# Rows of a DRAM scratch laid out for reads of 8 KB, written by 16 transfers in place of one

## The reference

```
def step(h, inp):
    x_t, dt_t, B_t, C_t = inp
    dA = jnp.exp(dt_t[..., None] * A)
    h = dA * h + (dt_t * x_t)[..., None] * B_t[:, :, None, :]
    y = jnp.einsum('bgpn,bgn->bgp', h, C_t)
    return (h, y)
```

## Time and profile before

| | |
|---|---|
| median of 3 runs | 1326.49 us (1325.91 to 1327.89) |
| the profiled execution | 1327.35 us, its span 1325.6 us |
| TensorE busy | 1094.1 us, 83% |
| VectorE busy | 1101.3 us, 83% |
| GpSimd busy | 977.7 us, 74% |
| ScalarE busy | 626.5 us, 47% |
| DMA packets | 99512, 98784 of them under 8 KB |
| mean granted TensorE clock | 0.919 |

### The profile page before, as it was taken

One profiled execution on the slowest core, in us unless ns is written; L12 is line 12 of the kernel. 1 busy time (PEld: TensorE's weight loads), 2 busy tenths in 40 slices (PEclk: granted clock), 3 DMA queues, 4 the chain that ended last, 5 costly groups with the idle time before them and its releaser, 6 DMA issues.

```text
span 1325.6 us, 14750 instructions
## 1 busy us (share of the span) xinstructions
PE 1094.1 (83%) x3848; PEld 551.6 (42%) x3848; DVE 1101.3 (83%) x1265; ACT 626.5 (47%) x1070; POOL 977.7 (74%) x596
## 2 busy tenths in 40 slices
PE   2476658999798987999698987999698988998888
PEld 1121123445344453435344453445344454445445
DVE  3389998899889998999889998999989998997222
ACT  3645455445554455545554454545554355442310
POOL 0489997877879786877888786877888788875100
PEclk9776779999899997999899997999899998999889
DMA  5797866655665657575756647574756557550000
GB/s 194 175 236 157 186 153 133 141 131 124 161 143 128 143 134 162 119 158 118 170 133 138 140 119 167 122 167 103 177 129 145 118 132 167 127 127 32 1 0 17
DMA packets 99512, 176.56 MB, mean 133 GB/s; under 512 B 12960, under 2 KB 21600, under 8 KB 98784
## 3 DMA queue, kind: packets, MB, share of 16 engines
q1 hardware_dynamic: 98272, 171.36, 56.2%
q0 software_dynamic: 1152, 4.19, 0.9%
HBM read 150.34 MB, written 8.39 MB: 120 GB/s over the span
## 4 chain that ended last, share of the span: by engine, by line
PE 34%; POOL 27%; issue 21%; ACT 7%; DVE 6%; DMA 3%; SPq 1%; POOLq 0%; DVEq 0%; ACTq 0%
POOL h_s L980 16%; PE p_r L456 9%; PE p_r L467 6%; PE p_r L462 6%; POOL bt_s L960 5%; PE p_dt L411 4%; PE p_y L422 3%; PE p_r L442 2%; DVE h_s L760 2%; DMA bt_s<-dx_rows 2%; PE p_r L473 2%; PE p_r L437 1%; ACT p_dt L549 1%; POOL carry L977 1%; POOL sp_l L994 1%
## 5 line engine op out<-in xcount | busy, mean ns | idle before, releaser
L980 POOL TENSOR_TENSOR h_s<-h_s,c_s 128x1024 f32<-128x1024 f32 x256 | 608.3, 2377 | 127.5 <-DVE h_s L760 117.2
L549 ACT ACTIVATE p_dt<-p_dt,an_s 128x512 f32<-128x512 f32 x512 | 333.1, 657 | 334.0 <-PE p_dt L411 333.5
L411 PE MATMUL p_dt<-kdt,pick_s 128*128 128x512 f32 x512 | 357.6, 704 | 106.9 <-DVE h_s L760 105.0
L760 DVE TENSOR_TENSOR_SCAN h_s<-p_dt,carry,bt_s 128x512 f32<-128x512 f32 x256 | 322.2, 1272 | 25.3 <-ACT p_dt L549 20.3
L760 DVE TENSOR_TENSOR_SCAN h_s<-p_dt,bt_s 128x512 f32<-128x512 f32 x256 | 304.9, 1210 | 31.0 <-ACT p_dt L549 17.7
L467 PE MATMUL p_r<-nT,w_s 128*128 128x512 f32 x512 | 243.2, 602 | 0.4 <-ACT nT L686 0.4
L960 POOL TENSOR_TENSOR bt_s<-bt_s,b_s 128x1024 f32<-128x1024 f32 x96 | 226.7, 2361 | 10.9 <-DMA bt_s<-dx_rows 10.5
L411 PEld LDWEIGHTS p_dt<-kdt,pick_s 128*128 128x128 f32 x512 | 103.4, 204 | 264.8 <-DVE h_s L760 180.7
L745 DVE TENSOR_TENSOR bt_s<-bt_s,p_b 128x1024 f32<-128x1024 f32 x160 | 192.7, 1204 | 4.5 <-issue 2.8
L456 PE MATMUL p_r<-nT,gu_s 128*128 128x512 f32 x352 | 169.4, 602 | 0.3 <-DVE th_s L905 0.3
L422 PE MATMUL p_y<-h_s,ysel_s 128*32 128x512 f32 x1024 | 150.6, 663 | 18.8 <-POOL h_s L980 18.8
(11 more groups left out here) (93 smaller groups left out, 900.7 us busy)
## 6 DMA issues: line engine op xcount, KB each, us to landing
bt_s<-dx_rows SPq DMA_DIRECT2D x512, 256.0 KB, 5.3
kdt<-st_dt SPq DMA_DIRECT2D x64, 128.0 KB, 3.2
tok<-in_x SPq DMA_DIRECT2D x8, 512.0 KB, 7.1
xr_s<-xb_s SPq DMA_DIRECT2D x64, 64.0 KB, 2.4
dx_rows<-sp_w SPq DMA_DIRECT2D x16, 256.0 KB, 2.0
b_s<-xb_s SPq DMA_DIRECT2D x64, 64.0 KB, 2.5
xo<-in_x SPq DMA_DIRECT2D x8, 512.0 KB, 3.9
out<-xo POOLq DMA_DIRECT2D x8, 512.0 KB, 3.4
```

Source lines behind the costliest of these rows:

```text
L411: nc.tensor.matmul(p_dt[DT_BANK[u]][:, :], sel, kdt[:, h, p // 16, :], start=True, stop=True)\
L549: A(p_dt[DT_BANK[u]][:, :], p_dt[DT_BANK[u]][:, :], ACT.Exp, scale=an_s[:, c:c + 1]).then_inc(a_dA, 1)
L760: V.tensor_tensor_scan(h_s[:, u % 8, :], p_dt[DT_BANK[u]][:, :], bt_s[:, u % 16, :], carry[:, u:u + 1] if par else 0.0, ALU.mult, ALU.add) ...
L980: G.tensor_tensor(h_s[:, two, :], h_s[:, two, :], c_s[:, h, :].unsqueeze(1).broadcast_to([P, 2, T]), ALU.mult)\
```

## The change

The scratch has a further layout: for each group and each of eight runs of a half, the four channels of the run stand one behind another, 4 x 512 x 4 B = 8 KB. A read still goes to 32 partitions and moves 256 KB, but takes one piece of 8 KB for each partition in place of four pieces of 2 KB that lie 64 KB apart. The write must put the eight channels of each pair (a, g) into that order and becomes 16 DMAs of 8 partitions (every fourth partition of `sp_w`), 16 KB each, in place of one of 128 partitions. The counts of `l_rows` go from 16 to 256 for each half.

```
-        dx_rows = nc.dram_tensor("dx_rows", [2, 2, P, T], F32).ap()
+        dx_rows = nc.dram_tensor("dx_rows", [2, 2, GH, 8, 4 * T], F32).ap()
...
-                p = unit_channel(4 * r)
...
-                kept_rows, scanned = number((t * 2 + h + 1) * 16), number(t * U + 4 * r - 12)
+                kept_rows, scanned = number((t * 2 + h + 1) * 256), number(t * U + 4 * r - 12)
...
                 for g in range(GH):
-                    src = dx_rows[par, h].rearrange("(a b g) t -> g b a t", a=4, g=GH)[g, p]
-                    sp.dma_start(bt_s[NS * g:NS * g + NS, slot:slot + 4, :], src.partition_broadcast(NS))\
-                      .then_inc(l_dx[r % 4], 16)
+                    sp.dma_start(bt_s[NS * g:NS * g + NS, slot:slot + 4, :].rearrange("p a t -> p (a t)"),
+                                 dx_rows[par, h, g, r % 8].partition_broadcast(NS)).then_inc(l_dx[r % 4], 16)
...
                 sp.wait_ge(g_dx, t * 2 + h + 1)
-                sp.dma_start(dx_rows[par, h], sp_w[:, :]).then_inc(l_rows, 16)
+                for a in range(4):
+                    for g in range(GH):
+                        sp.dma_start(dx_rows[par, h, g, :, a * T:a * T + T], sp_w[32 * a + g:32 * a + 32:GH, :])\
+                          .then_inc(l_rows, 16)
...
-                        act.wait_ge(l_rows, m * 16)
+                        act.wait_ge(l_rows, m * 256)
```

## The result

The changed kernel takes 1380.08 us in the median of 4 runs, the kernel before 1326.45: ratio 1.0402, 95% interval 1.0384 to 1.0420. That is 53 us more (4.0%); the prediction said 17 (range to 1359). The direction and the places were right, the size that it gave was a third of the measured one. The profiled execution has a span of 1376.2 us, 50.6 more than before.

The account below looks back on a forecast made before the run. Bound: the chain through ScalarE's `res`, delayed by late `xo` in SyncE's queue, with TensorE gapless later. 4.0 us at the start plus 13.0 at ends of tiles, 17.0 on 1327.35, less 0.86, gives 1343.5 us; range 1330 to 1359.

Parts of the forecast that it names:

- the sensitive place: SyncE's queue between a tile's last `keep_rows` (write of `dx_rows`) and the load of `xo`; a delay there delays the tile.
- the first run: Start: first four reads issued 7.35 us later, landing at 59.5 against GpSimd's start at 55.6; 4 us lost.
- The price of an issue: SyncE's queue: 0.49 us for each write, so 16 hold it 7.7 us in place of 0.38, 7.35 us more.
- the dear bound: SyncE's queue: all 16 writes as dear as SBUF to SBUF, 0.64 us each, 9.8 us more each time.
- working at the ends of tiles: Second half's writes delay `xo`: 7.35 us less each body's margin; lost 4.75, 3.8, 0.4 and 4.05, sum 13.0 us.
- The gain of the reads: Start: pieces of 8 KB land 5.2 us after first issue in place of 8.6, gain 3.4 us or 0; steady state 0.
- The second wait at the start: GpSimd's 4.2 us wait for a run behind the second write and 2 MB of weights; later issue and quicker reads cancel, 0.
- The middle of a tile: First half's writes: the next run goes out 2 us late, but its landing leaves 8 us before GpSimd; term 0.
- A stall of ScalarE counts in full: Ends of tiles: every microsecond ScalarE waits for `xo` lengthens the run, as the chain passes there and TensorE has no gap later.
- C: Rival, dear issues or slow reads: 9.8 us a group gives 1362 us, slow reads alone 1354; chance 0.18.
- A: Rival, issues cheap or covered: no measurable change, 1326.5 or up to 1329 us (1335 with 5.7 us each); chance 0.11.
- B: Rival, faster: GpSimd's second wait for reads at the start goes, 4.2 us won, 1322.3 us; chance 0.08.

Follow-up runs that it names:

- e9_xo_early_after: The changed kernel with a buffer of its own for the output and `xo` loaded at u = 44 of the body before: 1348.02 us, ratio 1.0139.
- e2_reads8k: The kernel before with the new layout and reads of 8 KB alone, still one write of 128 partitions: ratio 0.9987.
- e5_spread: The changed kernel with the second half's loads and writes moved in SyncE's queue behind the load of `xo` and one run of reads: ratio 1.0064.
- e6_forms: The kernel before (old layout) with 16 writes of 16 KB for each half, in several shapes tile by tile: 1373.73 us in one run.
- e14_w1_128: Reads of 8 KB with single writes, each 1 MB run read from weights w1 by one DMA into 128 partitions, not from the scratch: 1318.25 us, one run.
- e15_w1_32: Reads of 8 KB with single writes, each 1 MB run read from weights w1 by four DMAs of 32 partitions: 1325.15 us, one run.
- e8_xo_early: The kernel before with a buffer of its own for the output and `xo` loaded at u = 44 of the body before: ratio 0.9984.

## Why the prediction was wrong, step by step

**What bounds the kernel, and the sensitive place: right.** Late `xo` behind the second half's writes (`e9_xo_early_after`), the first run at the start, and no waiter for reads in the steady part (`e2_reads8k`). Moving the steps in the queue takes most of the loss away with every write still issued (`e5_spread`).

**The price of an issue: the step that failed most.** I took 0.49 us from the one write of before, which stood alone, with 0.64 (the SBUF to SBUF row) as the dear bound. Measured: 604 ns and a gap, 0.65 us, 10.3 us more for each group in place of 7.35, so even my dear bound was passed. I had argued that the shape doesn't set the price, since a larger transfer was the cheaper; `e6_forms` shows that the shape sets it, from 0.33 to 0.65 us at the same 16 KB. The loss is steep in this price, as the prediction said. Its own working at the ends of tiles with 10.3: 7.7 for body 1, 9.7 for 3 and 5, 7.0 for 7 and, by the margins of 2, 4 and 6, 8.3 at most, 32.7 us, in place of 13.0. Measured 28.3. Body by body the two agree less well, in us:

| body | by the working, at 10.3 | ScalarE's wait for `xo` grew by | VectorE's copies shorter by | lost |
|---|---|---|---|---|
| 1 | 7.7 | 7.6 | 2.3 | 3.5 |
| 2 | 3.0 | 4.0 | 0.5 | 4.2 |
| 3 | 4.9 | 6.2 | 2.7 | 3.6 |
| 4 | 2.0 | 3.1 | 0.2 | 3.3 |
| 5 | 4.9 | 5.1 | 2.9 | 2.9 |
| 6 | 3.3 | 5.2 | 1.1 | 2.8 |
| 7 and 8 | 7.0 | 7.9 | none there | 8.1 |

"Lost" is how much further behind the changed kernel is at the write ahead of the next body. Body 1 lost less than half of the working's figure, bodies 2 and 4 lost more than theirs; that the sums come so near is in part luck.

**The gain of the reads: failed.** 3.4 us counted, none measured at the start (8.7 us from issue to use, before 8.6). The 5.2 us of `pick` were no price for longer pieces but for 128 partitions (`e14_w1_128`, `e15_w1_32`). The estimate of 3% less, which I had worked out from the Trainium skill (DMA: Bandwidth & Descriptors, "Why small descriptors are slow") and set aside, is near what the traces show: 730 us of the engines' time with the reads of 8 KB alone, 745 before, and a packet of 8 KB takes 612 ns in the median where four of 2 KB take 616.

**The second wait at the start, set to 0: failed.** I had let later issue and quicker reads cancel. Nothing was quicker, and the group that stands in front of the fourth run is a second one, on top of the late start: 13.4 us in place of 4.2, so 9.2, above the 7.35 that I had given as its worst. With 9.7 for the first run (4 predicted) and 3.5 in the middle of tile 0, the start lost 22.3 us in place of 4. Two other waits are new at the start: ScalarE's for the written rows (8.5 us, to 52.07) and TensorE's for `kdt` (8.2 us, to 55.23). Both end ahead of GpSimd's first multiplication at 65.33, as I had said of the first.

**The middle of a tile at 0: right but for tile 0.** There GpSimd waited 3.5 us at 168.88, where I had read the margin off body 4 only.

**A stall of ScalarE counts in full: only in part.** The wait grew by 39.1 us and 28.3 us were lost. VectorE's copies, which had waited for GpSimd, became 9.6 us shorter at the same places, and that covers most of the difference. In body 7, which has no such copies, the wait counts in full, 7.9 us against 8.1. Of the 21.2 us that were there before, little counted (`e8_xo_early`): half of them lie in body 8 beside the output projection, which I had not looked up.

**The sum.** With what was measured for each term, 17.0 becomes 32.7 at the ends of tiles, 9.7 for the first run, 9.2 for the second wait and 3.5 in tile 0: 55.1 us against the 50.6 by which the span grew. The price of an issue is the largest part of the miss.

**Rivals.** C (dear issues or slow reads) came true in both parts at once, which the prediction priced only one by one (1362 and 1354), and with the second wait on top; a range that takes in bounds of several unknown costs has to allow for their sum. A and B were ruled out. (In A, 5.7 - 3.4 is 2.3 us, not 2.4; nothing hangs on it.)

## What to carry to other kernels

A queue's issue time is a resource like an engine's: before cutting one DMA in many, find what stands behind it in the queue, and price an issue by a row of the same shape, or measure that shape by itself. Steps that can wait belong behind the ones that are waited for: the same 256 writes cost 53 us in one order and 8.5 in another. A wait in the profile isn't worth its length: look for what ends next, and at durations that are out of proportion with the size of the instruction.

## What the runs showed of the hardware

- An issue of 16 KB from SBUF to DRAM holds SyncE's queue for 0.33 us (8 neighbouring partitions), 0.45 to 0.48 (16 x 1 KB, 32 x 512 B, 128 x 128 B) or 0.65 us (8 partitions with a step of 4, 64 x 256 B), gaps included.
- DMAs that fill 32 partitions each took the engines 55.3% of the span, one that fills 128 took 38.6%, for the same bytes.
- A packet of 8 KB takes 609 ns in the median when the DMA fills 32 partitions, 309 when it fills 128; four packets of 2 KB into 32 partitions take 616.
- A VectorE copy of 128 x 4 numbers lasts 0.16 us, or up to 5.29 us when GpSimd multiplies. The longest ones ended with the last of several GpSimd instructions that follow without a gap, not with the first.
